# A four-layer graph network on one core: scaled fp16 halves in place of three bf16 parts for the gathered tables and for layer 2's messages, and layer 2's one-hots made two chunks ahead

## The reference

```python
# layer 0: two hypergraph convolutions, relu between them
# layer 1: messages by an MLP over (edge features, receiver, sender), summed by receiver
edge_in = jnp.concatenate([edges, nodes[receivers], nodes[senders]], axis=-1)
h = jax.nn.relu(edge_in @ We1 + be1)
new_edges = h @ We2 + be2
agg = jax.ops.segment_sum(new_edges, receivers, num_segments=nodes.shape[0])
h2 = jax.nn.relu(jnp.concatenate([agg, nodes], axis=-1) @ Wn1 + bn1)
new_nodes = h2 @ Wn2 + bn2
# layer 2: gated messages, summed by receiver
k = x @ W_key + b_key;  q = x @ W_query + b_query;  v = x @ W_value + b_value
gate = jax.nn.sigmoid(k[dst] + q[src])
agg = jax.ops.segment_sum(gate * v[src], dst, num_segments=N_NODES)
return agg + x @ W_skip + b_skip
# layer 3: normalised sum over neighbours, no weights
```

## Time and profile before

| | |
|---|---|
| median of 3 runs | 4888.29 us (4879.47 to 4893.69) |
| profiled execution, span | 4870.2 us |
| PE busy | 4102.1 us, 84% |
| DVE busy | 3046.8 us, 63% |
| ACT busy | 1445.4 us, 30% |
| POOL busy | 2549.3 us, 52% |
| layer 1's edge pass | 1962 to 3478 us |
| layer 2's slot pass | 3655 to 4571 us |
| DMA | 1161 MB, mean 238 GB/s |

### The profile page before, as it was taken

One profiled execution on the slowest core, in us unless ns is written; L12 is line 12 of the kernel. 1 busy time (PEld: TensorE's weight loads), 2 busy tenths in 40 slices (PEclk: granted clock), 3 DMA queues, 4 the chain that ended last, 5 costly groups with the idle time before them and its releaser, 6 DMA issues.

```text
span 4870.2 us, 144047 instructions
## 1 busy us (share of the span) xinstructions
PE 4102.1 (84%) x56332; PEld 3693.9 (76%) x56332; DVE 3046.8 (63%) x4215; ACT 1445.4 (30%) x2353; POOL 2549.3 (52%) x2291
## 2 busy tenths in 40 slices
PE   0777799996999983899999998999759999999596
PEld 0666688886999983677777777777559898988496
DVE  5999888882111023677777776777447777777612
ACT  0333499991000003222222222222232222222100
POOL 0388866665656567776666665666003334333200
PEclk9777799998999996999999999999859999999798
DMA  5511388889999974677777776777317666666496
GB/s 170 212 30 30 114 320 324 321 319 306 399 379 418 417 287 165 209 243 235 237 238 239 239 236 220 239 240 240 126 28 247 222 204 220 224 226 204 144 407 257
DMA packets 430171, 1161.15 MB, mean 238 GB/s; under 512 B 111175, under 2 KB 250422, under 8 KB 422712
## 3 DMA queue, kind: packets, MB, share of 16 engines
q1 hardware_dynamic: 331478, 919.45, 53.5%
q0 software_dynamic: 66016, 114.12, 8.1%
q10 hardware_dynamic: 32256, 121.34, 6.4%
HBM read 791.79 MB, written 364.93 MB: 238 GB/s over the span
## 4 chain that ended last, share of the span: by engine, by line
PE 24%; DMA 24%; issue 23%; POOL 12%; DVE 12%; ACT 2%; POOLq 1%; ACTq 1%; SPq 1%; DVEq 0%
DMA feat_slot<-SK,sidx_p 18%; POOL arena L843 6%; POOL feat_slot L920 5%; PE PS L1357 5%; DVE arena L2407 4%; PE PS L1352 4%; PE PS L1363 4%; PE PS L1258 4%; PE PS L1383 2%; ACT arena L1756 2%; DMA sidx_p<-SK 1%; DVE arena L2359 1%; DVE arena L2342 1%; DMA arena<-feat_slot 1%; PE PS L1426 1%
## 5 line engine op out<-in xcount | busy, mean ns | idle before, releaser
L920 POOL DMA_INDIRECT feat_slot<-SK,sidx_p x900 | 1110.8, 1234 | 556.3 <-DMA feat_slot<-SK,sidx_p 283.9
L963 POOL DMA_INDIRECT arena<-tab_l_src,SK x864 | 975.4, 1129 | 470.4 <-DVE arena L2394 226.5
L843 POOL TENSOR_TENSOR arena<-arena 128x448 f32<-128x448 f32 x343 | 365.2, 1065 | 794.5 <-DVE arena L2299 794.5
L1426 PE MATMUL PS<-arena 128*128 128x128 bf16 x7203 | 648.9, 221 | 96.5 <-DVE arena L2342 58.6
L1258 PE MATMUL PS<-arena 128*128 128x192 bf16 (+1 forms) x7203 | 614.5, 248 | 104.7 <-DVE arena L2141 77.7
L1258 PEld LDWEIGHTS PS<-arena 128*128 128x128 bf16 x7203 | 606.0, 98 | 111.8 <-DVE arena L2141 62.1
L1357 PE MATMUL PS<-arena 128*128 (+1 forms) x6267 | 581.2, 221 | 37.0 <-DVE arena L2376 37.0
L1430 PE MATMUL PS<-arena 128*128 (+1 forms) x7203 | 610.5, 194 | 0.9 <-issue 0.9
L2407 DVE TENSOR_TENSOR arena<-arena 128x896 f32<-128x896 f32 (+1 forms) x319 | 329.1, 1032 | 405.3 <-ACT arena L1756 363.6
L1426 PEld LDWEIGHTS PS<-arena 128*128 128x128 bf16 x7203 | 455.7, 98 | 119.5 <-issue 109.6
L1741 ACT ACTIVATE arena<-PS 128x512 f32<-128x512 f32 (+1 forms) x319 | 175.2, 549 | 1091.2 <-PE PS L1363 1073.2
(11 more groups left out here) (254 smaller groups left out, 6683.7 us busy)
## 6 DMA issues: line engine op xcount, KB each, us to landing
arena<-slot_rows SPq DMA_DIRECT2D x343, 448.0 KB
arena<-cnt_t SPq DMA_DIRECT2D x147, 896.0 KB
hots<-arena ACTq DMA_DIRECT2D x175, 672.0 KB
arena<-hots SPq DMA_DIRECT2D x175, 672.0 KB
arena<-cnt_t SPq DMA_DIRECT2D x147, 672.0 KB
cnt_t<-arena SPq DMA_DIRECT2D x49, 1568.0 KB
cnt_s<-arena SPq DMA_DIRECT2D x49, 1568.0 KB
arena<-cnt_s SPq DMA_DIRECT2D x49, 896.0 KB
```

Of the source, the lines that this page charges most:

```text
L843: pool.tensor_tensor(hid3[i][:, 2 * n:3 * n], hid3[i][:, n:2 * n], upper3[i][:, n:2 * n], ALU.subtract)\
L920: pool.indirect_dma_start(feat_slot, bass.IndirectOffsetOnAxis(ap=sidx_p[odd][:, n:n + 1].bitcast(u32), axis=0), fwin[h][:, t * D:(t + 1) ...
L963: pool.indirect_dma_start(qgot[n % 3][:, slot_of[t] * P:(slot_of[t] + 1) * P], None, tab_src[4], bass.IndirectOffsetOnAxis(ap=gidx[odd][:, ...
L1426: last = nc.tensor.matmul(PS[:, to:to + P], selS[c][:, cut], qsplit[:, (b * 3 + s) * H:(b * 3 + s + 1) * H], start=s == 0, stop=False, ski ...
```

## The change

1. The tables of layers 1 and 2 are split in two fp16 parts in place of three bf16 parts. fp16 has more bits but a narrow range, so the weights that make the tables (`wpq`, `wtwo`, `we1`'s first part, `wkq`) are first multiplied by powers of two found from bounds on the result (`scale_up`; more steps in `fold_weights`, with one more fp32 product of 448 columns), and the scale is undone in `wfold`, in the sigmoid (`scale=`), and where layer 2's sum is added. A slots item has 28 table matmuls, a natural one 12. Layer 1's messages stay in three bf16 parts.
2. Layer 2's messages are two fp16 halves. ACT makes the first, by a new copy (`first_half`), which it issues behind the next chunk's sigmoid; GpSimd makes the second by its one subtraction. VectorE's `residual` is gone, `add_up` has 128 columns, and `second_part` is two operations.
3. In layer 2 VectorE makes the one-hots of an odd block two chunks ahead, those of chunks 0 and 1 in turns 5 and 6 of the even block before. VectorE's loop is peeled at its end as well (`tail=True`, 6 turns of 6 blocks).

```diff
-        qsplit = carve(0, NB * 3 * H, bf16)
-        dsplit = carve(36.75, NB * 3 * H, bf16)
-        qrest = carve(100, NB * H)
+        qsplit = carve(0, NB * 2 * H, f16)
+        dsplit = carve(36.75, NB * 2 * H, f16)
...
+        gated = [carve(122.5 + 3.5 * i, CH * D) for i in range(3)]
+        halves = [carve(124.25 + 3.5 * i, 2 * CH * D, f16) for i in range(3)]
...
-                        pool.wait_ge(msg_res, w * NC + (PLACES + c + 1))
-                        pool.tensor_tensor(hid3[i][:, 2 * n:3 * n], hid3[i][:, n:2 * n], upper3[i][:, n:2 * n], ALU.subtract)\
-                            .then_inc(msg_lo, 1)
+                        pool.wait_ge(msg_hi, w * NC + (c + 1))
+                        pool.tensor_tensor(halves[i][:, n:2 * n], gated[i], halves[i][:, 0:n], ALU.subtract).then_inc(msg_lo, 1)
...
-                            for s in range(3):
-                                nc.tensor.matmul(PS[:, to:to + P], selp[c % 4][:, cut], qsplit[:, (of * 3 + s) * H:(of * 3 + s + 1) * H],
+                            for s in range(2):
+                                nc.tensor.matmul(PS[:, to:to + P], selp[c % 4][:, cut], qsplit[:, (of * 2 + s) * H:(of * 2 + s + 1) * H],
...
-                        for s in range(3):
+                        for s in range(2):
                             last = nc.tensor.matmul(PS[:, to:to + P], selS[c][:, cut],
...
+                def first_half(w, c, odd):
+
+                    i = (c + odd) % turns
+                    act.wait_ge(pre_free, w * NC + (NS * NC + c + 1))
+                    nc.scalar.activation(halves[i][:, 0:CH * w_], gated[i], ACT.Copy).then_inc(msg_hi, 1)
...
                     for c in range(NC):
                         messages(w, c, odd)
+                        if c >= 1:
+                            first_half(w, c - 1, odd)
+                        elif not first:
+                            first_half(w - 1, NC - 1, (odd - 1) % turns)
...
+                V.tensor_tensor(wsq[:, 0:2 * H], wpq[:, :], wpq[:, :], ALU.mult)
...
+                TS(wpq[:, :], wpq[:, :], up[0], None, ALU.mult)
...
-                    with dve.Fori(0, NC) as c:
-                        at = bass.ds(c * CH, CH)
-                        dve.wait_ge(splits_mid, c + (1 + NC * (2 * m + i)))
-                        V.tensor_tensor(s3[:, at, 2, :], r3[:, at, :], s3[:, at, 1, :], ALU.subtract).then_inc(splits_lo, 1)
+                        V.tensor_tensor(s3[:, at, 1, :], t3[:, at, :], s3[:, at, 0, :], ALU.subtract).then_inc(splits_lo, 1)
...
                         if old:
                             gate(*old)
-                        if not kept:
-                            select_rows(w, c, j)
-                        if old:
-                            residual(*old)
-                        if not kept:
-                            select_sums(w, c, j)
+                        if kept and not last and c >= NC - AHEAD:
+                            select(w + 1, c - (NC - AHEAD), j)
+                        if not kept and c < NC - AHEAD:
+                            select(w, c + AHEAD, j)
                         if c == 4 and not first:
                             second_part(w - 1)
```

More of the change, by code:

```diff
@@ L113, in carve @@
             a = int(kb * 256)
-            size = {f32: 4, i32: 4, bf16: 2}[dt] * n
+            size = {f32: 4, i32: 4, bf16: 2, f16: 2}[dt] * n
             b = a + -(-size // 4)
@@ L149, in build @@
         epsc = sb("epsc", [P, 2])
+        wsq = carve(100, 2 * H + 3 * D, parts=D + 1)
+        bound = sb("bound", [P, 3])
+        scale_i = sb("scale_i", [P, 6], i32)
+        scale_up = scale_i[:, 0:3].bitcast(f32)
+        scale_down = scale_i[:, 3:6].bitcast(f32)
+        wnorm = sb("wnorm", [D + 1, 1])
         XT = carve(114, NB * P)
@@ L479, in chunk_of, with blocks @@
             return slice(o * CH, (o + 1) * CH)
-        def blocks(eng, body, turns=2):
+        def blocks(eng, body, turns=2, tail=False):
+            if turns == 3 and tail:
+                for u in range(7):
+                    body(u, u % 3, u // 2, u % 2 == 0, first=u == 0)
+                with eng.Fori(1, (NB - 1) // 6 - 1) as i:
+                    for r in range(1, 7):
+                        body(i * 6 + r, r % 3, i * 3 + r // 2, r % 2 == 0)
+                for u in range(NB - 6, NB):
+                    body(u, u % 3, u // 2, u % 2 == 0, last=u == NB - 1)
+                return
             if turns == 3:
@@ L1827, in _ @@
             step(V.memset(gcol[:, :], 0))
+            V.memset(wnorm[0:D, :], float(D))
+            step(V.memset(wnorm[D:D + 1, :], 1.0))
             step(V.memset(XA[:, :, D:D + 1], 1.0))
```

108 lines of the change are left out of this document (57 added, 51 removed).

## The result

The changed kernel takes 4730.32 us (median of 4, 4708.64 to 4742.94), the kernel before 4883.88 us (median of 4, the runs shown above and one more). The ratio is 0.9692, 95% interval 0.9657 to 0.9726: faster by 3.1%. The forecast was 4542 us, and its range of 4430 to 4660 does not hold the result.

What follows compares the result with a forecast made beforehand. It took a closed chain through ACT, VectorE and PE to bound the edge pass and PE to bound layer 2; −138 − 4.5 − 204 = −346.5 off 4870.2, plus 18.1, gave 4542 us, range 4430 to 4660.

Steps and rivals of the forecast that it cites:

- closed chain in the edge pass: Edge pass: ACT's copy, VectorE's one-hot and PE wait on each other in turn; the cycle falls from 9.38 to 8.57 us.
- the ring: Layer 2: sigmoid, copy, GpSimd, sum and table product close over two items; 1.96 us per item, or 2.11.
- The rival of two passes: Table matmuls: a 16-bit operand of the new type costs two passes, 0.116 us per product; 5238 us, chance 0.04.
- Start: Before the edge pass: VectorE's new scaling operations, at most 7 us, are covered by its wait for indices; 0.
- Splits for layer 2: Splitting of layer 2's second table: one difference per chunk ends it at 3646.4 instead of 3650.85; −4.5 us, bounds 0 and −9.
- Edge pass: −138 forecast: Layer 1's edge pass: 28 table matmuls for 42 take 5.6 us off each pair, to 56.4, times 24.6 pairs.
- the border stretch: Edge pass, items at a pair's border: fewer matmuls save 3.1 us at most, 2.4 taken per pair.
- The bound of −90: Edge pass, smallest gain: gathers, late behind VectorE, hold each pair of blocks at 58.4 us.
- Layer 2: −204 forecast: Layer 2's slot pass: 24.5 pairs of 28.5 us plus 14 give 712 us against 916.
- The one-hots now come two chunks ahead: Layer 2: the lead covers PE's waits for the one-hot, 0.9 us at a block border, 3.7 at a loop's.
- longer chain and late gathers: Both passes: items of 2.2 us, 4 us per loop border, and gathers as edge-pass bound; about 4655 us, chance 0.20.
- The clock rival: PE's idle gaps lower its clock to 1.2 GHz: layer 2 alone about 4930 us, edge pass too above 5500; chance 0.04.

Runs made afterwards that it cites:

- e9: Changed kernel with seven one-hot and slot-feature buffers in the edge pass in place of four, a semaphore for each; 4613.54 us, ratio 0.9427.
- e8: Changed kernel with layer 2's sigmoid given the constant scale 1.0 in place of the column of scales; 4724.36 us in one run.
- e3: Changed kernel with row loads for an odd block's chunks 0 and 1 issued before the even block's one-hot loads of chunks 5 and 6; 4661.19 us.
- e11: Changed kernel with layer 2's pass in loop turns of 12 blocks in place of 6; 4693.81 us, ratio 0.9598.
- e10: Changed kernel with seven edge-pass buffers with own counters, layer 2's rows asked for earlier, and loop turns of 12 blocks; 4555.55 us, ratio 0.9321.
- e4: Changed kernel with GpSimd's subtraction in layer 2 cut to 8 of 448 columns from the fourth chunk on; 4626.62 us, ratio 0.9501.
- e2: Changed kernel with layer 2's one-hots made one chunk ahead in place of two; 4669.98 us, ratio 0.9564.
- e5: Changed kernel with ACT's stores of the one-hots in the edge pass cut to 64 of 2688 columns; 4602.31 us, ratio 0.9435.

## Why the prediction failed, point by point

**What bounds the kernel.** The closed chain in the edge pass, and PE as the bound of layer 2's items, were read rightly: with 28 instead of 42 table matmuls the cycle became 8.61 us (forecast 8.57), and when GpSimd was taken out of the ring an item was 1.64 us (forecast 1.60). An fp16 product costs what a bf16 one does: table products of layer 2 start 55 ns apart in the median before and after. The rival of two passes falls. The Trainium skill, "FP8 and Floating Point Precision", section "TensorE Precision Notes", has BF16 and FP16 brought to the same inner format and gives four passes to true FP32 alone; this trace agrees.

**Start and splits.** Start 0: of the five us by which the first copy is earlier 1.6 reach the pass, whose first natural item PE starts at 1960.47 us instead of 1962.05, since it waits for GpSimd. Splits for layer 2: −4.5 forecast, about −7 measured once the clock's 23 us are set aside.

**Edge pass: −138 forecast, −42 measured.** The step that failed is "In the border stretch three slots items and two natural ones lose 3 × 0.81 and 2 × 0.35 … I take 2.4". The border gained nothing: four cycles gave 3.1 us per pair, and the stretch became 1 us longer (62.15 − 3.1 + 1.0 = 60.05, instead of 56.4). I had costed PE, ACT, VectorE and GpSimd in this pass and left SyncE out. Its loads wait for the store of the one-hots that lie in the buffer; the chunks are seven and the buffers four, so at a pair's border a buffer comes round after three slots items instead of four. Before, the wait was hidden behind PE, with 22 us showing over the pass; when PE ran faster it became 84 us. The bound of −90 "if gathers … hold each pair" was for the wrong resource, and too tight on that side. With the wait mended (e9) the pair took 56.77 us.

That this is so near to the forecast's 56.4 is in part luck. It is the mean of two kinds of pair: in e9 those with a loop turn in them take 59.2 us and the others 54.0, in the changed kernel 62.9 and 56.9, and before 63.6 and 60.5. The change thus took 3.6 us off a pair without a turn and 0.7 off one with it. The sum worked from one pair of 62.05 us and had no term for the turn in this pass, though it had one in layer 2. In the changed kernel a turn costs some 1.4 us more than before, at ten borders; the larger part of the shortfall is the wait that e9 took away.

**Layer 2: −204 forecast, −86 measured.** The ring is right in kind and nearly in size: 2.04 us per item against 1.96 in the even blocks, 2.10 against 2.11 in the odd ones. Two of its terms were mis-sized. The sigmoid takes 0.63 us for 0.54, through the scale column (e8: 13 us over the pass). GpSimd's subtraction, taken from the kernel before as 0.93 in even blocks and 1.25 in odd ones, has a median of 1.03 to 1.04 in both; why was not tested. With these two the sum's ring gives (2.50 + 1.60)/2 = 2.05 us per item, and the good fit in the odd blocks is partly that two errors cancel. The step that failed is the sentence "The one-hots now come two chunks ahead …, so the waits for L2342 … have cover". The lead needs its rows two chunks earlier, and the same sum had them arriving in time without a look at SyncE's order: the loads of the odd block's rows stand behind those of the even block's last two chunks, each of which waits for a sum of PE. Nor did the sum say who stands behind VectorE's wait; it is the gates. The excess is 7.7 − 4.1 = 3.6 us at each of 24 borders, 86 us, where it had been 6.2 − 4.8 = 1.4 before. The second part is "of the seven loop borders I keep 2 us each": six show, and they cost 6 × (11.6 − 7.7) = 23 us on top, against 14. Of the first, e3 took away 64 us; of the second, e11 took four turns of six.

**DMA.** Costed at 0, with +30 as the far bound. No run shows the rate as a bound: e10 moves 258 and 265 GB/s through the two passes at a DMA share of 0.81 and 0.76, and e4 272 in layer 2; the 286 that the sum asked for were never needed. When a transfer is asked for, and what it waits for, was the larger part of both misses.

**The rivals.** The nearest was the first, longer chain and late gathers, about 4655. Its time was nearer than the forecast's, and still 75 us too low, for neither the wait for the store nor that for the rows was in it. Its loop turns are real: in layer 2 a turn costs 3.6 us before (9.8 against 6.2), 3.9 in the changed kernel and up to 6.3 in e2 (10.7 against 4.4). The Trainium skill, "Runtime: NRT & Kernel Launch", section "Instruction fetch mechanics", says that a taken branch to a target outside the two loaded pages forces a fetch before execution goes on; e11 shows that the turn costs the time, not that the fetch is its cause. That gathers hold a pair is not borne out: in e5 and e9 pairs of 55.6 and 56.8 us leave room for them. The clock rival came true in part: 0.93 in layer 2 against 0.99, with the falls beside the long gaps at the borders. With most of those gaps mended it was 0.98 in e10, although PE still stood idle some 250 times in 343 items, for 0.5 us in the median. The Trainium skill, "TensorE: Matmul & The Clock Gate", section on depth-cycling of the PSUM queue, has brief idling between groups of matmuls move the clock up and down; e10 does not bear that out for idle times of this length.

What no run settles: how the difference of 333 us in e10 splits exactly between the mendings, since the profiled spans hold the clock's 23 us in some and not in others; by the passes it is 151 us for the edge pass (last copy 3473.8 to 3323.2) and 161 for layer 2, and the rest lies between them and in the spread of the runs.

## What to carry to other kernels

When an engine that hid everything gets faster, redo the sum for every queue, the one that only issues transfers first: for each load, what it waits for, what stands before it, and when its data is needed. A lead of n steps for a consumer is a lead of n steps for its loads as well, and a waiting instruction on an in-order engine holds what is unrelated behind it. And where a ring of buffers does not divide the loop's count, its real depth is the shortest distance, found at the border.

## What the runs showed of the hardware

- A VectorE operation with 128x1792 bf16 elements takes 0.68 us with GpSimd nearly silent (e4) and up to 1.49 beside GpSimd's subtraction of 128x448; in the timeline of the changed kernel one that starts at 3761.26, 0.03 us behind GpSimd's of 1.03 us, takes 1.48. The Trainium skill, "SBUF — State Buffer", section on the two separate sides, has the two engines share a port pair that is locked for a whole instruction. This trace agrees in kind; in size a full wait for GpSimd's end and 0.68 us behind it would be 1.68 us, 0.2 more than measured.
- ACT's sigmoid of 128x448 takes 0.63 us with a column of scales and 0.54 with a constant.
- Where a loop turns, the kernels here lose 3.6 to 6.3 us in layer 2 (e11 shows the turn as the cause) and 2 to 4.4 us in the edge pass (not shown by an experiment).
- The same program runs a stretch of fp32 products at 1.2 GHz in one execution and at 2.4 in another; in the kernel before PE was busy for all 32 us of the window shown and the clock did not rise. What decides was not found. A stage's time between two kernels should be compared only after a look at its clock.
